# A graph network on one core: some block sums from gathered source rows in place of dense counts

## The reference

```python
h = jnp.maximum(_layernorm(x), 0.0)              # x: 6250 x 128
# src, dst: 206250 edges (100000 both ways, and a loop on each node), sorted by dst
def _sage_conv(x, src, dst, Wl, bl, Wr):
    agg = segment_sum(x[src], dst) / max(count, 1)
    return agg @ Wl.T + bl + x @ Wr.T
h = relu(batch_norm(_sage_conv(h,  Wl0 256x128 ...), gamma0, beta0))   # layer 0
h = relu(batch_norm(_sage_conv(h,  Wl1 256x256 ...), gamma1, beta1))   # layer 1
h = _sage_conv(h, Wl2 128x256 ...)                                     # layer 2
return x + log_softmax(h)
```

## Time and profile before

| | us |
|---|---|
| median of 3 runs | 1513.04 (1510.34 to 1513.68) |
| the profiled execution's own time | 1508.48 |
| its span | 1506.7 |
| layer 0, with its last block | 0 to 549 |
| transition with the heads of layer 1 | 549 to 610.2 |
| layer 1, 23 blocks | 610.2 to 1173.8 |
| transition with the heads of layer 2 | 1173.8 to 1228.0 |
| layer 2, 23 blocks, and the end | 1228.0 to 1506.7 |
| PE / DVE / ACT / POOL busy | 1418.1 / 616.1 / 544.1 / 120.0 |

### The profile page before, as it was taken

One profiled execution on the slowest core, in us unless ns is written; L12 is line 12 of the kernel. 1 busy time (PEld: TensorE's weight loads), 2 busy tenths in 40 slices (PEclk: granted clock), 3 DMA queues, 4 the chain that ended last, 5 costly groups with the idle time before them and its releaser, 6 DMA issues.

```text
span 1506.7 us, 31846 instructions
## 1 busy us (share of the span) xinstructions
PE 1418.1 (94%) x14074; PEld 1280.7 (85%) x14074; DVE 616.1 (41%) x954; ACT 544.1 (36%) x1298; POOL 120.0 (8%) x81
## 2 busy tenths in 40 slices
PE   1499999999999989999999999999999899999997
PEld 1388898988898979899999999999999898888886
DVE  6998898989898943100000000000000222112212
ACT  4897979897878747100000000000000430000001
POOL 2323131313130000000000000000000000000000
PEclk9999999999999999999999999999999999999999
DMA  5244454545454422434343333334340358888882
GB/s 165 88 165 157 158 189 189 189 183 195 180 198 175 176 95 86 140 128 160 122 151 130 132 130 132 130 132 141 126 161 10 93 223 305 285 302 289 300 286 99
DMA packets 49914, 252.24 MB, mean 167 GB/s; under 512 B 7790, under 2 KB 31532, under 8 KB 34796
## 3 DMA queue, kind: packets, MB, share of 16 engines
q1 hardware_dynamic: 47372, 243.59, 45.4%
q0 software_dynamic: 2400, 6.56, 1.5%
HBM read 168.50 MB, written 81.62 MB: 166 GB/s over the span
## 4 chain that ended last, share of the span: by engine, by line
PE 80%; DVE 10%; ACT 5%; issue 3%; DMA 2%; POOL 1%; DVEq 0%; SPq 0%; POOLq 0%; ACTq 0%
PE bank L802 62%; PE bank L795 6%; DVE hots L621 5%; PE bank L810 4%; PE bank L813 4%; ACT ring L459 2%; DVE parts L621 2%; PE bank L1237 2%; PE bank L1439 1%; DMA parts<-in_pairs_dram,first_i 1%; ACT junk L412 1%; PE bank L1226 1%; POOL parts L351 0%; PE bank L1450 0%; ACT Z L436 0%
## 5 line engine op out<-in xcount | busy, mean ns | idle before, releaser
L802 PE MATMUL bank<-ring,parts 128*128 128x250 f16 x9800 | 1121.3, 270 | 1.3 <-DVE agm L630 1.1
L802 PEld LDWEIGHTS bank<-ring,parts 128*128 128x128 f16 x9800 | 937.6, 97 | 100.9 <-issue 1.6
L459 ACT CAST ring<-bank 128x490 f16<-128x490 f32 x625 | 322.8, 587 | 81.6 <-PE bank L795 79.1
L621 DVE TENSOR_TENSOR hots<-iotas,tab 128x2560 f16<-128x2560 f16 (+1 forms) x232 | 277.3, 1245 | 1.5 <-ACT tab L420 0.8
L1277 ACT ACTIVATE Z<-bank,vec 128x250 f32<-128x250 f32 x48 | 19.9, 466 | 529.5 <-PE bank L813 529.5
L630 DVE SCALAR_TENSOR_TENSOR agm<-bank,bnw,rcb 128x250 f32<-128x250 f32 x50 | 21.5, 473 | 375.4 <-PE bank L802 375.4
L795 PE MATMUL bank<-hots 128*128 128x98 f16 x2080 | 136.7, 212 | 33.3 <-DVE hots L621 30.8
L795 PEld LDWEIGHTS bank<-hots 128*128 128x128 f16 x2080 | 120.3, 99 | 47.1 <-DVE hots L621 36.4
L621 DVE TENSOR_TENSOR parts<-iotas,tab 128x2560 f16<-128x2560 f16 (+1 forms) x118 | 139.4, 1222 | 2.2 <-ACT tab L420 1.2
L1397 ACT ACTIVATE junk<-rows_i 128x128 f32<-128x128 f32 (+1 forms) x49 | 14.7, 301 | 253.0 <-DVE rows_i L1426 253.0
L693 DVE BATCH_NORM_STATS2 st<-Z 128x6 f32<-128x250 f32 x96 | 35.2, 408 | 152.8 <-ACT Z L1277 152.3
(11 more groups left out here) (118 smaller groups left out, 541.3 us busy)
## 6 DMA issues: line engine op xcount, KB each, us to landing
c_blocks<-ring SPq DMA_DIRECT2D x25, 3062.5 KB, 10.6
ring<-c_blocks SPq DMA_DIRECT2D x46, 1562.5 KB, 6.5
ring<-c_blocks SPq DMA_DIRECT2D x46, 1500.0 KB, 6.6
rcb<-rc_row SPq DMA_DIRECT2D x75, 125.0 KB, 7.7
Z<-in_x_dram SPq DMA_DIRECT2D x4, 768.0 KB, 6.7
out_dram<-rows_i SPq DMA_DIRECT2D x24, 128.0 KB, 5.3
smp_i<-in_samples_dram SPq DMA_DIRECT2D x1, 403.0 KB, 3.3
rows_i<-in_dst_rows_dram,row_i POOLq DMA_INDIRECT x25, 4.0
```

Of the source, the lines that this page charges most:

```text
L459: act.copy(blk[c % 2][:, :, d0:d0 + GD * GPK].rearrange("p a (g d) -> p a g d", d=GD), bank[(0, 1, 5, 6)[(2 * t + h) % 4]][:, 0:GPK * NW] ...
L621: ins = dve.tensor_tensor(o[:, 0:q, :, :], iota2[:, 0:w, :].unsqueeze(1).to_broadcast((P, q, w, 2)), place.unsqueeze(2).to_broadcast((P, q ...
L802: return pe.matmul(bank[b][:, 0:BD], view[0:r, a, part, m * P:m * P + P], blk[c % 2][0:r, a, :], start=(a, part) == (0, 0), stop=(a, part) ...
```

## The change

Blocks 18 to 22 (`loose`) are left out of the dense lists of layer 1, and blocks 18 and 19 out of those of layer 2; the dense orders close up, and the two ring slots are given out by position (`slot_of`). Their sums come from gathered rows instead. Each block is two windows of 125 destinations, each window four groups of 31 or 32 (`WIN`), and the edges of a group, which lie together, are cut into 9 tiles of 128 (10 for the fourth group, `WT`). At each transition SP also stores the layer's f16 features, high and low part side by side, as a table of 6250 rows in HBM: 1 KB a row in layer 1, 512 bytes in layer 2. POOL gathers one tile of 128 source rows with each indirect DMA, into one of two sets of five tiles. A **round** is the tile `t` of all four groups (the ninth round has a fifth tile): PE multiplies a one-hot of 128 edges x 32 destinations (weights) with the 128 x 512 (or 256) gathered rows and writes partitions 32j to 32j+31 of one bank. After nine rounds VectorE adds the two parts and scales (`dve_group_mean`), PE turns the result (`pe_group_turn`), ScalarE copies it (`act_gmean`), and after two windows the linear part of the block follows. `take`, `fold`, `turn_at`, `lin_at` and `hot_at` place this in the step count of the dense loop: 90 rounds from step 37 to step 842 of 882 in layer 1, 36 rounds from step 49 to step 914 of 1029 in layer 2.

In layer 0, from about step 150 of 325, the sources and positions of the 40 groups' edges are found once: two more indirect DMAs with 40 rows each, signs and passes over 1280 elements on ScalarE, some 25 mostly tiny operations on VectorE, twenty transposes of 40 x 128 on PE. The flag also tests that no group has more edges than places.

```diff
-    orders = [list(range(NB)), list(range(NB))[::-1], list(range(NB))]
+    loose = list(range(NB - 2 - NG1, NB - 2))
+    gathered = [[], loose, loose[0:NG2]]
+    rounds = [[(n, k, t) for n, k in enumerate(wins[layer]) for t in range(RPG)] for layer in range(3)]
+    rowf = [0, 512, 256]
+    def tiles_of(t):
+        return [(t, j) for j in range(4)] + ([(t + 1, 3)] if t == RPG - 1 else [])
...
+    begin = [0, NA - NA // 4, NA]
+    spans = [0, NA * (len(orders[1]) - 2) - 12, NA * (len(orders[2]) - 2) - 40]
+        nh = len(rounds[layer]) + 2
+        at = [begin[layer] + (spans[layer] - begin[layer]) * h // nh for h in range(nh)]
+        for r in range(len(rounds[layer])):
+            take[layer].setdefault(at[r], []).append(r)
...
+        def table_store(layer, view, a0, a1):
+            for b0, b1, r in ((a0, min(a1, FULL), P), (FULL, a1, LAST)):
+                if b0 < b1:
+                    sp.dma_start(tables[layer][b0 * P:b0 * P + (b1 - b0) * r, :].rearrange("(a p) f -> p a f", p=r),
+                                 view[0:r, b0:b1, :, :].rearrange("p a s f -> p a (s f)")).then_inc(d_table[layer], 16)
...
+        def pool_round(layer, r):
+            n, k, t = rounds[layer][r]
+            if r >= 2:
+                pool.wait_ge(t_round, rbase[layer] + r - 1)
+            else:
+                pool.wait_ge(d_table[layer], table_dmas)
+            for i, (tile, j) in enumerate(tiles_of(t)):
+                o = 40 * k + 4 * tile + j
+                pool.indirect_dma_start(
+                    out=got[layer][:, 5 * (r % 2) + i, :], out_offset=None, in_=tables[layer],
+                    in_offset=bass.IndirectOffsetOnAxis(ap=src_i[:, o:o + 1], axis=0)).then_inc(d_got[r % 2], 16)
...
+        def dve_group_hot(layer, n):
+            dve.tensor_tensor(ghot(layer, n), iota2[:, 0:32, :].unsqueeze(1).to_broadcast((P, 20, 32, 2)),
+                              at.unsqueeze(2).to_broadcast((P, 20, 32, 2)), ALU.is_equal).then_inc(v_ghot, 1)
+        def dve_group_mean(layer, n, own):
+            dve.wait_ge(t_round, RPG * (gbase[layer] + n + 1))
+            dve.tensor_scalar(mean, b[:, 0:F], rcg[:, k:k + 1], None, ALU.mult).then_inc(v_own, 1)
+            dve.wait_ge(v_own, own.up())
+            dve.scalar_tensor_tensor(mean, b[:, F:2 * F], rcg[:, k:k + 1], mean, ALU.mult, ALU.add).then_inc(v_gsum, 1)
...
+        def pe_round(layer, r):
+            n, k, t = rounds[layer][r]
+            b = bank[sum_bank[layer]]
+            if t == 0:
+                if gbase[layer] + n:
+                    pe.wait_ge(v_gsum, gbase[layer] + n)
+                pe.wait_ge(v_ghot, gbase[layer] + n + 1)
+            pe.wait_ge(d_got[r % 2], landed[layer, r])
+            g = ghot(layer, n)
+            for i, (tile, j) in enumerate(tiles_of(t)):
+                ins = pe.matmul(b[32 * j:32 * j + 32, 0:rowf[layer]], g[:, 2 * tile + j // 2, :, j % 2],
+                                got[layer][:, 5 * (r % 2) + i, :], start=(tile == 0), stop=(tile == WT[j] - 1))
+            ins.then_inc(t_round, 1)
...
         def sync_layer1():
-            for k in range(2):
-                block_load(1, 2, k)
-                block_load(1, 3, k)
+            for k in range(4):
+                if k == 2:
+                    block_load(1, 2, 0)
+                    block_load(1, 3, 0)
+                if k == 3:
+                    block_load(1, 2, 1)
+                table_here(a_hi1, v_lo1, 2, xcuts[k + 1])
+                table_store(1, wide, xcuts[k], xcuts[k + 1])
+            block_load(1, 3, 1)
...
         def pe_layer1():
-            for j in range(2, NB):
+            for j in range(2, D1):
...
+                    for b in dense_lin[1].get(t, []):
+                        pe_product1(b)
+                    for n in turn_at[1].get(t, []):
+                        pe_group_turn(1, n)
+                    for b in lin_at[1].get(t, []):
+                        pe_product1(b)
+                    for r in take[1].get(t, []):
+                        pe_round(1, r)
...
         def sync_layer2():
-            for k in range(2):
-                block_load(2, 2, k)
-                block_load(2, 3, k)
+            for k in range(4):
+                if k == 2:
+                    block_load(2, 2, 0)
+                    block_load(2, 3, 0)
+                    block_load(2, 2, 1)
+                    block_load(2, 3, 1)
+                table_here(a_hi2, v_lo2, 4, xcuts[k + 1])
+                table_store(2, small, xcuts[k], xcuts[k + 1])
```

More of the change, by code:

```diff
@@ L26 @@
 NTAB = 8
+NG1 = 5
+NG2 = 2
+WIN = 31
+WT = (9, 9, 9, 10)
+WE = 1280
+RPG = 9
+NEAR = 3
 class Tally:
@@ L1261, in sync_layer1, with pool_layer1 @@
                              .rearrange("(a p) f -> p a f", p=r)).then_inc(d_xres, 16)
+        def pool_layer1():
+            for r in range(len(rounds[1])):
+                pool_round(1, r)
         def act_layer1():
@@ L1379, in sync_layer2, with pool_layer2, act_logs @@
                 sp.wait_ge(d_out[s], 16 * len(range(s, len(units), 4)))
+        def pool_layer2():
+            for r in range(len(rounds[2])):
+                pool_round(2, r)
+        def act_logs(j):
+            for u in ends[j]:
+                a0, n, r, _ = units[u]
+                act.wait_ge(v_dd, u + 1)
+                for i in range(n):
+                    act.activation(ex[0:r, i, :], dd[0:r, u % 4, i, :], ACT.Exp,
+                                   accum_out=sm[0:r, 1, a0 + i:a0 + i + 1]).then_inc(a_exp, 1)
+                act.wait_ge(a_exp, unit_acts[u])
+                act.activation(sm[0:r, 2, a0:a0 + n], sm[0:r, 1, a0:a0 + n], ACT.Ln).then_inc(a_log, 1)
         def act_layer2():
@@ new lines, in act_layer2, with dve_add @@
+            act_logs(D2)
+        def dve_add(b):
+            i = lins[2].index(b)
+            dve.wait_ge(t_lin2, i + 1)
+            if b in gathered[2]:
+                dve.wait_ge(a_gmean, gmeans_upto(2, gathered[2].index(b)))
+                mean = agmg[:, 0, :]
+            else:
+                v = visit_of[2][b]
+                dve.wait_ge(v_mean, v + 1)
+                mean = agm[:, v % 2, 0, :]
+            dve.scalar_tensor_tensor(Z[:, 0, BD * b:BD * b + BD], bank[7][:, 0:BD], bias[2][:, 0:1],
+                                     mean, ALU.add, ALU.add).then_inc(v_z2, 1)
@@ new lines, in dve_finals @@
+        def dve_finals(j, own):
+            for u in ends[j]:
+                a0, n, r, _ = units[u]
+                v = bank[u % 3][0:r, 0:P * n].rearrange("p (a f) -> p a f", a=n)
+                dve.wait_ge(t_fin, u + 1)
+                if u >= 4:
+                    dve.wait_ge(d_out[u % 4], 16 * (u // 4))
+                dve.tensor_reduce(sm[0:r, 0, a0:a0 + n], v, AX.X, ALU.max).then_inc(v_own, 1)
+                dve.wait_ge(v_own, own.up())
+                dve.tensor_tensor(dd[0:r, u % 4, 0:n, :], v,
+                                  sm[0:r, 0, a0:a0 + n].unsqueeze(2).to_broadcast((r, n, P)),
+                                  ALU.subtract).then_inc(v_dd, 1)
+                dve.wait_ge(a_log, u + 1)
+                dve.wait_ge(d_xres, 32)
+                for i in range(n):
+                    dve.scalar_tensor_tensor(dd[0:r, u % 4, i, :], dd[0:r, u % 4, i, :],
+                                             sm[0:r, 2, a0 + i:a0 + i + 1], xres[0:r, a0 + i, :],
+                                             ALU.subtract, ALU.add).then_inc(v_fin, 1)
@@ new lines, in dve_layer2 @@
+            dve_mean(vbase[2], [agg_bank2(o2[0])], isp)
+            dve_mean(vbase[2] + 1, [agg_bank2(o2[1])], isp)
+            for j in range(2, D2):
+                for a in range(NA):
+                    t = NA * (j - 2) + a
+                    for n in hot_at[2].get(t, []):
+                        dve_group_hot(2, n)
+                    for b in products(2, t - 3):
+                        dve_add(b)
+                    for n in fold[2].get(t, []):
+                        dve_group_mean(2, n, own)
+                    if a == FIN + 2:
+                        dve_finals(j, own)
+                dve.wait_ge(v_z2, lins[2].index(o2[j - 2]) + 1)
+                dve_mean(vbase[2] + j, [agg_bank2(o2[j])], isp)
@@ L1490, in gnn_program @@
             sync_layer1()
+            pool_layer1()
             act_layer1()
```

533 lines of the change are left out of this document (397 added, 136 removed).

## The result

The changed kernel took **1532.6 us** (median of four runs, 1530.4 to 1539.5), the kernel before, on the same chip, 1512.5: a ratio of 1.0142 (1.0108 to 1.0177). It is slower by 1.4%; the forecast was 1473, and the time lies at the upper end of the range. On another chip it is slower still, by 5.3% (further down). The profiled execution has a span of 1531.0 us against 1506.7.

What follows compares the result with a forecast made beforehand. After layer 0 the time was taken as a count of PE matmuls. From 1508.5 us, +4 (layer 0), -52 (layer 1) and +8.5 (layer 2) gave 1469, with the median's 4.5 more 1473; range 1446 to 1535.

Steps and rivals of the forecast that it cites:

- Layer 1, what PE must do: Layer 1: PE's remaining dense matmuls, linear parts, 90 rounds of 0.50 us and transposes sum to 506.6 us.
- drained on both sides: Rival, layers 1 and 2: shape changes drain PE before and after each round, 0.66 us a round, 1490 us; chance 0.13.
- one after the other: Rival, layers 1 and 2: the four column groups do not overlap, rounds 0.90 and 0.44 us, 1507 us; chance 0.12.
- Layer 1, POOL: Layer 1: 370 indirect DMAs at a pitch of 1.26 us, 466 us in all, POOL ending at 1088.
- The rival that ended slower: Rival, layer 1: POOL's gathers miss the 1.26 us pitch, nothing gained above 1.40; at 1.57, 1579 us; chance 0.20.
- I add 5 us for it: 1122: Layer 1: allowance over PE's own end at 1116.8 for POOL's near-equal pace and uneven linear parts, giving -52 us.
- some 3 us: Layer 1: time for the last gathered tile to land after POOL ends, 4.0 us from issue less the 0.95.
- Layer 2: Layer 2: +8.5 us (-6 to +29), two blocks fewer against 36 rounds and a 14 us wait before the first.
- the half: Layer 0: half the sum of DVE's 6.7 us and PE's 2 us of added work, +4 us (0 to 14).
- some 4 that I added from the profiled execution to the median: Whole kernel: the median of 1513.04 lay 4.5 us above the profiled execution, raising the sum from 1469 to 1473.

Runs made afterwards that it cites:

- e3: Changed kernel with each half-block load of layers 1 and 2 cut to one source tile, leaving most counts out of the sums; 1487.0 us, 0.9856 of the kernel before.
- e4: Changed kernel with three blocks gathered in layer 1 and none in layer 2; 1483.8 us, 0.9835 of the kernel before.
- e1: Changed kernel with no block gathered and no table stored, all layer 0 preparation kept; 1522.5 us, 1.0092 of the kernel before.
- e9: As e1, without the preparation's second half (window gather, conversion, mask, count, place, twenty transposes); 1517.3 us, 1.0054 of the kernel before.
- e5: As e4, with four steps of layer 0's preparation on ScalarE and VectorE moved later; 1490.0 us, 0.9859 of the kernel before.
- e2: Changed kernel with five blocks gathered in layer 1 and none in layer 2; 1519.4 us, 1.0072 of the kernel before.
- e13: The changed kernel repeated unaltered on chip 7; 1586.2 us, 1.0531 of the kernel before.
- e7: Changed kernel with four blocks gathered in layer 1 and none in layer 2; 1485.6 us, 0.9839 of the kernel before.
- e14: Repeat of the changed kernel with layer 2's rounds begun 12 steps later; 1584.8 us.
- e11: Changed kernel with layer 2's first round at step 108 in place of 49 and half-block loads cut to one source tile; 1575.7 us, 1.0448 of the kernel before.

## Why the prediction was wrong

**Layer 1, what PE must do: right.** 506.6 us forecast, 505.8 measured in e3. A round was put at 0.50 us and is about 0.45 to 0.49. Four one-hots of 32 columns do stream together; drained on both sides or one after the other fell.

**Layer 1, POOL: right.** The pitch of 1.26 held for 370 gathers wherever POOL did not wait for PE (mean 0.96 us busy, 0.30 between), with the DMA engines at 0.57. The first came 12.4 us into the layer, 11.8 forecast. The rival that ended slower expected a pitch over 1.40; it named the DMA load, but as a thing that slows the issuing.

**Layer 1, "I add 5 us for it: 1122": this step failed.** It took a landing of "some 3 us", the median of layer 0's indirect DMAs, as a constant. The kernel before showed that it is none, for the 25 gathers of L342, from issue to landing:

```profile
DMA to landing us min/median/max: 2.6/4.0/8.6
```

Of all 50, the nine slowest (6.2 us and more) lay beside transfers of SP's queue that took 0.44 to 0.67 of the engines' time; the quickest took 2.5. In layer 1, next to block loads, the data came 2 to 7 us behind the end of the issue. The 5 us also had to cover a ring of two rounds between an issuer of 5.18 us and a taker of 5.17, where each late round holds up POOL too, since it may not overwrite the set. Measured: 52 us over PE's own 505.8, in place of 5. 32.7 of them come from the block loads (21.5 late data, 11.2 clock), shown by e3; the 19 that e3 still waits I put down to pace and two sets. e4 shows the cure from the other side: with slack in POOL all of it goes.

**Layer 2: right in its main term.** One wait of 12.96 us before the first round (14 forecast, 10 to 17). The stage lost 12.8 us, 8.5 forecast. The rest is four short waits, 3.7 us in sum, and 2.1 more at the end, where the last linear part now waits 4.5 us for VectorE instead of 2.4.

**Layer 0: the half was mis-sized.** I took half of VectorE's and PE's work, 4 us, on the strength of their idle shares. It was 13.9 by e1 and 17.3 in the profiled execution. The sum had no term for waits. The trace of e9 has 8.8 us of them in one stretch, where VectorE asks ScalarE and GpSimd for results in turn, against 6.7 of added VectorE work in all. How the 13.9 us divide between work and waits stays open, since e5, which took one of the waits away, gained nothing.

**The sum.** The miss is 60 us: 46 in layer 1 (-52 forecast, -6 measured), 13 in layer 0, 4 in layer 2, less some 4 that I added from the profiled execution to the median and that the new kernel does not show (its profiled execution took 1533.5).

**On chip 7** even this sum is not the last word: the same kernel takes 50 us more in layer 1. No row of the kernel before could show that, since it has no long stretch of gathers.

## What to carry to other kernels

Price a gather in three numbers: the issuer's pitch, the landing next to the bulk loads of that very stage, and how many rounds of buffer lie between them. Here issuer and taker had the same pace, and a late landing was not made up; take fewer units, so that the issuer has slack (here three blocks in place of five turned e2's +0.7% into e4's -1.7%). Repeat a result on several chips, and on one chip at several times, before believing a per cent or two, above all when the change makes GpSimd issue DMAs without a pause.

## What the runs showed of the hardware

- **A bulk load starves gathers.** For stretches of 2 us SP's queue had 90% of the 16 engines or more and POOL's queue 5.4% or less, at 648 to 650 us nothing. The Trainium skill ("DMA: Bandwidth & Descriptors", Queues, rings and completion order) says that an engine goes round the queues packet by packet; the packets counted here from 674 to 676 us, 58 of SP's queue and 9 of POOL's, are far from even. Whether POOL's queue had packets ready on the engines all that time is not seen.
- **The same kernel differs from place to place.** In all 13 kernels with gathers run on chips 1, 2, 4 and 7 PE's instruction stream has gaps that nothing releases (1.5 to 62 us), in those of chip 3 and in the first comparison none. e9, without gathers, has none on chip 4, and the kernel before takes the same on all. In such a place one to five dense matmuls come every 0.7 or 1.4 us, for 1 to 10 us. Most follow stretches of about seven or more gathers without a pause. Short block loads, the order of PE's later instructions and the tables' place did not matter. The Trainium skill ("Runtime: NRT & Kernel Launch", Instruction fetch mechanics) says that an engine fetches its instructions by DMA and that the cost is mostly hidden. Late instructions would look like these rows, but no run here shows that it is this. The DMA trace speaks rather against it: its instruction queue q8 moved 109 packets (1.79 MB) in the changed kernel as in e13, in layer 1 one every 16 to 17 us, of about 1 us each in both, and the gaps of e13 lie at any distance behind the last of them, 0 to 20 us. Each chip was used in one session only, so whether the gaps belong to the chip or to the session stays open too.
- **Column groups stream together**: four matmuls of 32 weight columns by 512 in 0.40 us, a fifth 0.22 more.
- **A GpSimd TENSOR_SCALAR of 128 x 512 took 6.92 us** where its like took 1.93. In the kernel before that is the first of its five. In all 19 kernels with the added steps it is the third, which has the added gather of 40 rows 7 us ahead of it; in 15 of them also the first (in e2, e4, e7 and e14 that took 1.94), and in e11 the fifth. Why is not shown.
